# Recurrent layer with a gated FFN on 8 cores: order of the first loads, of the x tiles, of the first kvg product and of the weight sums

## The reference, cut to what matters

```python
# x: (4, 4096, 1024); Wq, Wk, Wv: (1024, 64); Wo: (64, 1024); Wg: (1024, 1)
# w_gate, w_up: (3072, 1024) int32; w_down: (1024, 3072) int32
xn = (x - mean(x)) / sqrt(var(x) + 1e-5)
q, k, v = xn @ Wq, xn @ Wk, xn @ Wv
gates = sigmoid(xn @ Wg + bg)
decay = 0.9 + sigmoid(decay_param) * 0.099
# over the tokens t of a row, from S = 0:
#   S = decay * S + (k_t g_t)^T (v_t g_t);  out_t = q_t S
s = outs @ Wo + bo
h = silu(xn @ (w_gate / 127).T) * (xn @ (w_up / 127).T)
g = silu(h @ (w_down / 127).T)
out = x + s * g
```

## Time and profile before

| | |
|---|---|
| median of 3 runs | 559.07 us (557.17 to 561.91) |
| profiled execution | 560.54 us, its span 559.0 us (core 6, the slowest) |
| spans of the 8 cores in it | 550.6 to 559.0 us |
| busy in the span | PE 523.1 us (94%), DVE 303.9 (54%), ACT 173.5 (31%), POOL 93.5 (17%) |
| chain that ended last | PE 83%, DMA 8%, DVE 4%, issue 3%, POOL 1%, ACT 1% |

### The profile page before, as it was taken

How to read it: one execution, slowest core, us unless ns; L and a number is a source line. 1 busy time by engine, 2 the same in 40 slices (tenths; PEclk the granted TensorE clock), 3 DMA queues, 4 the chain that set the end, 5 groups by cost and what they waited for, 6 DMA issues and landing times.

```text
span 559.0 us, 8459 instructions; the slowest of 8 cores (550.6 to 559.0 us)
## 1 busy us (share of the span) xinstructions
PE 523.1 (94%) x2765; PEld 249.3 (45%) x2784; DVE 303.9 (54%) x622; ACT 173.5 (31%) x274; POOL 93.5 (17%) x157
## 2 busy tenths in 40 slices
PE   0749999999989899999999999999999999999996
PEld 0336544445444344445554444444444444444442
DVE  4276876656656744566555366666666554221222
ACT  2331445444443321333200344333333432011010
POOL 2232442222322710010000031111111000000000
PEclk9978999999999989999999999999999999999999
DMA  5965989999999957173222244654544400322231
GB/s 160 188 142 72 166 119 140 161 175 154 160 161 169 184 109 177 45 234 111 76 85 86 75 76 77 92 90 82 77 75 80 72 1 2 119 89 94 92 116 56
DMA packets 28074, 62.04 MB, mean 111 GB/s; under 512 B 3135, under 2 KB 3263, under 8 KB 28032
## 3 DMA queue, kind: packets, MB, share of 16 engines
q0 software_dynamic: 18672, 36.19, 42.6%
q1 hardware_dynamic: 9216, 25.17, 14.0%
q10 hardware_dynamic: 144, 0.14, 0.1%
HBM read 89.28 MB, written 8.39 MB: 175 GB/s over the span
## 4 chain that ended last, share of the span: by engine, by line
PE 83%; DMA 8%; DVE 4%; issue 3%; POOL 1%; ACT 1%; DVEq 0%; POOLq 0%; ACTq 0%; SPq 0%
PE bank L335 44%; PE bank L397 29%; DMA gu<-wgu 5%; DMA xs<-xtm 3%; PE bank L448 2%; PE bank L417 1%; PE bank L431 1%; DVE bst L565 1%; PE bank L467 1%; DVE bst L566 1%; PE bank L328 1%; PE bank L321 1%; POOL t L923 1%; ACT xnt L816 1%; PE bank L502 0%
## 5 line engine op out<-in xcount | busy, mean ns | idle before, releaser
L397 PE MATMUL bank<-wd,hT 128*128 128x512 bf16 x749 | 168.0, 379 | 1.1 <-issue 0.2
L335 PE MATMUL bank<-xs,S_w 128*128 128x512 f16 x552 | 139.8, 379 | 2.6 <-DVE bank L763 2.6
L397 PEld LDWEIGHTS bank<-wd,hT 128*128 128x128 bf16 x768 | 74.7, 98 | 89.0
L335 PE MATMUL bank<-xnT,gu 128*128 128x512 f16 x368 | 94.5, 379 | 0.1
L335 PEld LDWEIGHTS bank<-xs,S_w 128*128 128x128 f16 x552 | 52.0, 98 | 62.8 <-issue 2.7
L886 POOL DMA_DIRECT2D gu<-wgu x48 | 26.2, 546 | 261.5 <-DVE S_w L539 143.2
L797 DVE TENSOR_TENSOR sg_all<-sg_all,bank 128x512 f32<-128x512 f32 x32 | 21.9, 685 | 76.8 <-ACT sg_all L878 76.7
L878 ACT ACTIVATE sg_all<-bank 128x512 f32<-128x512 f32 x32 | 19.1, 595 | 123.8 <-PE bank L397 123.8
L335 PEld LDWEIGHTS bank<-xnT,gu 128*128 128x128 f16 x368 | 34.5, 98 | 40.6 <-issue 1.0
L335 PE MATMUL bank<-xs,gu 128*128 128x512 f16 x184 | 48.2, 385 | 3.3 <-DVE m L773 3.2
L552 DVE SCALAR_TENSOR_TENSOR hT<-bank,sg_all 128x512 bf16<-128x512 f32 x69 | 47.3, 688 | 6.6 <-PE bank L335 5.5
(11 more groups left out here) (106 smaller groups left out, 461.3 us busy)
## 6 DMA issues: line engine op xcount, KB each, us to landing
gu<-wgu POOLq DMA_DIRECT2D x96, 256.0 KB, 5.6
xs<-xtm SPq DMA_DIRECT2D x16, 512.0 KB, 6.1
xr<-xtm SPq DMA_DIRECT2D x16, 512.0 KB, 3.8
out<-xr SPq DMA_DIRECT2D x32, 256.0 KB, 2.0
wd<-wdt POOLq DMA_DIRECT2D x24, 256.0 KB, 12.6
xr<-xpfm POOLq DMA_DIRECT2D x8, 512.0 KB, 14.5
wa<-wall POOLq DMA_DIRECT2D x1, 388.0 KB, 7.9
con<-cst ACTq DMA_DIRECT2D x1, 139.0 KB, 6.5
```

The source lines that it names most:

```text
L335: mm = pe.matmul(out=out[:], lhsT=weight(d), rhs=moving(d), start=(start and d == 0), stop=(d == 3), skip_group_check=True)
L397: mm = pe.matmul(out=bank[2 * (i % 2) + dh][:], lhsT=hT[:, hcols(hc, (i % 8) * 128, 128)], rhs=wd[:, hc * 1024 + dh * 512:hc * 1024 + dh * ...
```

## The change

Four things are moved; no instruction of compute or load is added or removed.

1. GpSimd issues chunk 0 when token tile 0 has landed, ahead of the power of tile 0; the small weights `wa` follow behind that power, chunk 1 behind tile 1's, chunk 2 behind tile 3's and the decay power instead of behind tile 4's.
2. SyncE issues x tile 4 when tile 0 is normalised, 5 when tile 1 is, and so on.
3. `kvg` 0 stands ahead of `plain` 0, and the others of the first half move up one place each; the wait for `wa` goes from `cw` to `kvg` 0. `decay_1` stands two transposes earlier.
4. S1 of the next pair is made behind the first h product of q3, S2, S3 and S4 behind the last. TensorE waits for S1 at the head of each q0 and for S2 at the head of each q1, in every window. `px_gates_2` goes from behind q1 to behind q2 of window 10.

```diff
-    order += [("decay_0", 0), ("stats", 0), ("stats", 1), ("norm", 0), ("gu_load", 0),
...
+    order += [("decay_0", 0), ("gu_load", 0), ("stats", 0), ("wa_load", 0), ("stats", 1), ("norm", 0),
...
-    slots[41] += [("px_gates_2", 0)]
+    slots[42] += [("px_gates_2", 0)]
...
                 if q == 0:
-                    if first:
-                        pe.wait_ge(ld_gate[2 * g % NGU], gu_loads(2 * g))
-                        pe.wait_ge(ld_up[2 * g % NGU], gu_loads(2 * g))
+                    pe.wait_ge(dve_S, 4 * w + 1)
...
                     product(W_A[0], A(0, 1, 1), B(1, 1), True).then_inc(pe_m1, 1)
-                    if first:
-                        pe.wait_ge(dve_S, 4 * w + 1)
...
                 elif q == 1:
-                    if first:
-                        pe.wait_ge(dve_S, 4 * w + 2)
+                    pe.wait_ge(dve_S, 4 * w + 2)
...
                 elif stage == "cw":
-                    pe.wait_ge(ld_wa, 16)
...
                 elif stage == "kvg":
+                    if i == 0:
+                        pe.wait_ge(ld_wa, 16)
...
             def S1(g):
+                wait_weights(g, 1)
                 wait_weights(g, 2)
...
             def S2(g):
-                wait_weights(g, 1)
...
                     if q == 1:
-                        if following:
-                            v.wait_ge(pe_m5, 2 * w + 2)
-                            S1(g + 1)
                         for m in range(2):
...
-                        if following:
-                            S2(g + 1)
...
-                        if following:
-                            S3(g + 1)
                     elif q == 3:
...
                         h_of(g, 2, 2, m5[1][:], sg[1])
+                        if following:
+                            v.wait_ge(pe_m5, 2 * w + 2)
+                            S1(g + 1)
...
                         h_of(g, 2, 1, W_A[1][:], sg[0])
                         if following:
+                            S2(g + 1)
+                            S3(g + 1)
                             S4(g + 1)
...
                 if stage == "gu_load":
+                    if i == 0:
+                        g.wait_ge(ld_x[0], 16)
                     load_gu(i)
...
                     elif i >= NXS:
-                        y.wait_ge(act_norm, 4 if i < 8 else i - NXS + 1)
+                        y.wait_ge(act_norm, i - NXS + 1)
```

More of the change, by code:

```diff
@@ L40, in stage_order @@
     order = [("x_load", i) for i in range(NXS)]
-    order += [("decay_0", 0), ("stats", 0), ("stats", 1), ("norm", 0), ("gu_load", 0),
-              ("stats", 2), ("norm", 1), ("tr", 0), ("wa_load", 0),
-              ("stats", 3), ("norm", 2), ("gu_load", 1), ("tr", 1), ("norm", 3),
-              ("tr", 2), ("tr", 3), ("decay_1", 0)]
-    order += [("x_load", i) for i in range(4, 8)]
-    order += [("plain", 0), ("stats", 4), ("gu_load", 2), ("norm", 4), ("h", 0),
+    order += [("decay_0", 0), ("gu_load", 0), ("stats", 0), ("wa_load", 0), ("stats", 1), ("norm", 0),
+              ("x_load", 4), ("gu_load", 1), ("stats", 2), ("norm", 1), ("x_load", 5), ("tr", 0),
+              ("stats", 3), ("norm", 2), ("x_load", 6), ("tr", 1), ("norm", 3), ("x_load", 7),
+              ("decay_1", 0), ("tr", 2), ("tr", 3), ("gu_load", 2)]
+    order += [("kvg", 0), ("plain", 0), ("stats", 4), ("norm", 4), ("h", 0),
               ("stats", 5), ("gu_load", 3), ("norm", 5), ("stats", 6)]
-    order += [("plain", 1), ("tr", 4), ("kvg", 0), ("norm", 6), ("h", 1), ("stats", 7),
-              ("tr", 5), ("kvg", 1), ("norm", 7), ("tr", 6), ("kvg", 2),
-              ("gu_load", 4), ("tr", 7), ("kvg", 3)]
+    order += [("plain", 1), ("tr", 4), ("kvg", 1), ("norm", 6), ("h", 1), ("stats", 7),
+              ("tr", 5), ("kvg", 2), ("norm", 7), ("tr", 6), ("kvg", 3),
+              ("gu_load", 4), ("tr", 7)]
     order += [("plain", 2), ("TS_0", 1), ("h", 2), ("kvg", 4), ("px_load", 0)]
```

## The result

The changed kernel takes 555.5 us (median of 16 runs) against 559.1 us for the kernel before (16 runs); the ratio is 0.9931, 95% interval 0.9914 to 0.9948. The forecast was 551.0: the direction was right, the gain of 3.6 us (3.9 by the ratio) was a little under half of the 8.1 us forecast. Four of the changed kernel's 16 runs took 577 to 636 us, with cores of one die at a lower clock; the ratios leave such runs out.

The account below looks back on a forecast made before the run. TensorE was taken as the bound, with time to win at the start and in first-half stalls. Core 6: 559.0 - (4.8 + 2.0 + 2.5) = 549.7; core 0, 549.8, plus 1.54 less 0.3 gave 551.0 us; range 547.0 to 556.5.

Parts of the forecast that it names:

- Start: Up to the third projection: earlier x tiles and `kvg` 0 bring the h product 4.8 us sooner; bounds 5.5 us and nothing.
- rival 1: At the start: `wa` lands after 24 us, TensorE stands at `kvg` 0, start wins nothing; 555.8 us, chance 0.10.
- Weight sums: First-half windows: with S1 out of q1, late chunks no longer hold the adds; 2.0 us, between 0 and 3.1.
- gates: Window 10: with the gates' chain behind the q2 adds, the S0 product starts sooner; 2.5 us, between 1.0 and 3.9.
- Rival 2: Windows 4 to 9: loads stay the bound, the stall only moves to the window's head; 553.0 us, chance 0.12.
- its sign: Waits of TensorE appearing at the heads of windows 6 to 9 with the DMA share at 1.
- Rival 3: Gates' stall moves to the S0 product and first `recur`, shown by 2 us or more at S0; 553.5 us, chance 0.12.
- Rival 4: Window heads: S1 ends late behind an h product needing ACT's silu, making the kernel slower; 568.2 us, chance 0.04.
- the waits at 0: Waits added on TensorE at each q0 and q1 cost 0; tightest room 0.25 us, in the second half.
- The base: Core 0's forecast span 549.8, plus 1.54 us around the profiled span, less 0.3 us towards the median: 551.0.
- core 6's own sum: Core 6's span of 559.0 less the three terms 4.8, 2.0 and 2.5: 549.7 us.

Follow-up runs that it names:

- e4_fill: Changed kernel plus seven idle 512-column matmuls behind each of `kvg` 1 and 2, filling TensorE's two long start waits; ratio 0.9869 to the kernel before.
- e11: Kernel before with only `px_gates_2` moved from slot 41 to 42; no ratio, cores 0 to 3 had spans 1.9 us less on the mean.
- e7: Changed kernel with `px_gates_2` put back in its old slot, all else as changed; ratio 0.9917 to the kernel before.
- e5: Changed kernel with the first part of the prefix gates one slot earlier, away from S1; ratio 0.9911 to the kernel before.
- e1: Kernel before with only the new start (order, x loads, waits), windows as before; gain 0.0028 by the ratio, interval to 1.0004.
- e8: Kernel before plus eight idle 512-column matmuls behind `kvg` 0; ratio 0.9992 to the kernel before.
- e6: Changed kernel with later down-weight loads, 14 idle matmuls at the start and the first gates part one slot earlier; 549.6 us, ratio 0.9834 to the kernel before.
- e2: Changed kernel with the start of before, keeping the moved weight sums and gate slot; gain 0.0041 by the ratio to the kernel before.
- e3: Changed kernel with down-weight loads spread later, so that windows 1 to 11 load less; ratio 0.9902 to the kernel before.
- e9: Changed kernel with `kvg` 0 to 3 back behind the plain products; third projection at 40.8 us, window 1 at 49.2 us.
- e10: Changed kernel with x tiles 4 to 7 issued behind tile 3 as before, other start edits kept; ratio 0.9891 to the kernel before.

## Why the prediction was right or wrong

**Start, forecast 4.8 us: the mechanism right, the size 2.6 on the slowest core.** h product forecast at 26.7, seen at 26.45; third projection forecast at 40.6, seen at 40.90; cost of waiting for `wa` inside the 0.7 us I had taken, rival 1 refuted. The step that failed is the silent assumption that a third projection 4.6 us sooner means a window 1 as much sooner. On core 3 window 1 began at 51.17 against 53.76 on core 6 before: 2.6 us. The other 2.0 are the halved clock (3.57 + 2.24 against 1.89 + 1.89), and `e4_fill` shows it: with the waits filled nothing is late. I had written that the list between held the same work, which is true of its instructions and not of their speed. The term was also read from single cores: the mean gain of the eight at window 1 is 3.1 in this pair of executions and 2.3 over all executions of either start.

**Weight sums, forecast 2.0, and gates, forecast 2.5: each about right alone, wrong as a sum.** Between the slowest cores the stretch shrank by 160.84 - 157.09 = 3.75 us, on the mean by 3.05, not by 4.5. Alone, the gates' move gives about 2 (`e11`); the rest of the change without it gives all 3.05 (`e7`), and the move on top 0.1 by its waits. The step that failed is adding them. Once S1 and S2 are out of q1, VectorE reaches the gates earlier, the stall on the add is 1.6 us and no longer 2.7, and no lower clock follows it (on none of eight cores). The term for the gates was also put together from two errors that nearly cancel. I forecast 4.5 us (195.0 - 190.52) from the last q2 product to the S0 product, and 191.85 - 187.28 = 4.57 was seen, where 7.64 had been. But the 1.3 us of clock in those 7.64 were not in my count of the stall, and such a loss doesn't come in each execution (15 of the 24 cores of the three with the old windows), and what came back, 0.96 at the S0 product and 0.48 at the next head, sits in TensorE's waits, where I had expected little.

**Rival 2 (loads stay bound, the stall moves to the window head) happened in part.** Core 3 waited 1.2 us each at the heads of windows 8 and 9 with the DMA share at 1.01, as its sign was given, on two of eight cores (3 and 5); on the other six such a wait was absent. I had put the chain in the text for one window (square, silu, h product, S1) and taken 2.0 of 3.1 us for it; the prefix piece was later on core 3 (5.41 us of waiting against 4.34 in the earlier trace rows). A stall that I had not listed at all is the 0.70 at window 10's head: part 0 of the gates stands in the slot ahead of S1, as `e5` shows by removing it.

Late chunks as such did not hold S1: no weight sum waits for a chunk on any core. The median landing of a chunk is 6.0 to 7.5 us over the cores, where it was 5.4 to 6.4: some 0.4 us longer on the mean, and no run here says what makes it longer. The rule of the Trainium skill that the prediction quotes for x tiles (DMA: Bandwidth & Descriptors, section "Queues, rings and completion order"), from which the prediction worked out that an x tile issued alone should land sooner, is not borne out: the four tiles landed in 8.5 to 15.0 us on core 3, where they had taken 10.2 to 12.8 on core 6, and over the cores the longest of the four took 12.0 to 15.1 us, where it had taken 11.1 to 13.3. What comes sooner is their issue.

**Rival 3 half.** The S0 product waited 0.96 us, under the 2 I had set.

**Rival 4 and the waits at 0: right.** 344.6 and 344.7 us from the first down product to the end; the 0.25 us of room in the second half was enough.

**The base.** The terms came from the slowest core of an execution that was 1.4 us above its median, and I took 0.3 of it off. The changed kernel's profiled execution was 0.9 below its median. Of the 4.5 us by which 551.0 fell short of 555.5, 3.3 are the spans (549.8 forecast, 553.1 seen), and 1.2 the step from a span to the median (1.54 - 0.3 = 1.2 added, 2.4 needed). On core 6's own sum the spans differ by 9.3 - 5.9 = 3.4 us: 2.2 are the start, 0.75 the windows, and 0.4 lie behind the first down product, which takes 344.4 us on core 6 and 344.8 on core 3. That last part and the step to the median are the luck of which core and which execution was looked at.

## What to carry to other kernels

When work that fed TensorE is brought forward, read the granted clock of the stretch that comes sooner, and what waits stand ahead of it: here the gain stayed whole only where the matmuls there still ran at full clock, and a few idle matmuls in two long waits held it. Two edits that relieve the same queue are not worth their sum: price the second in the kernel that has the first, or put each back alone. And with eight cores that differ by 8 us, read each term on all of them, and in more than one execution: means over eight cores still moved by 1 us between executions whose code was the same up to that point.

## What the runs showed of the hardware

A stall of 2.2 to 2.7 us in the middle of a full stretch was followed by slower matmuls on 15 of 24 cores (before, `e1`, `e8`), at 1.2 to 1.7 us more (granted clock 0.70 over 4 us on core 6); on the other nine, with stalls of 2.21 to 2.56 us, by none. Its length alone doesn't decide it. Stalls of 1.56 us at the same place were followed by none on eight cores (`e7`).

The same list of instructions went into the third projection at the lower level on 23 of 40 cores and at the full one on the rest; seven filler matmuls in each of two waits made it full on all 16 of `e4` and `e6`.

A third kind of slowness has no stall ahead of it: in `e1`, `e2`, `e3`, `e4`, `e7` and `e8` (and on cores 4 to 7 of `e11`) two to six cores were granted 0.81 to 0.94 of full speed for 4 to 20 us with TensorE busy throughout, most often from 52 to 60 us; neighbours (0 and 1, 2 and 3, 4 and 5) had it together. The profiled executions of before, the changed kernel, `e5`, `e6`, `e9` and `e10` show none. It lengthens a stretch by up to 2.5 us (cores 4 and 5 of `e3`), so the stretches of two kernels, one with it and one without, differ by more than their edits.
